# One PSUM tile in place of three, and the next chunk's layer norm ahead of three tiles, in a two-layer recurrent block

## The reference

```python
xn = layernorm(x)                                # layer 0
k, v, r = xn @ Wk.T, xn @ Wv.T, sigmoid(xn @ Wr.T)
kv = k * v                                       # scan over the 4096 positions:
#   wkv_t = state + exp(time_first) * kv_t ; state = decay * state + kv_t
s = (r * wkv) @ Wo.T
h = silu(xn @ wg.T) * (xn @ wu.T)                # 3072 wide, weights int / 127
g = silu(h @ wd.T)
x = x + s * g
xn = layernorm(x)                                # layer 1
diffs = xn[1:] - xn[:-1]                         # 8 of them in a window
normed, mag = diffs / |diffs|, |diffs|
gw = softmax(2 * cos(normed, guidance))          # 512 guidance vectors
blended = 0.6 * normed + 0.4 * gw @ guidance
w = pos_weight * tanh(2 * mag)                   # over the window of 8
s = sum(blended * w) / sum(w)
g = silu(xn @ ternary(weight).T * scale)
out = x + s * g
```

## Time and profile before

| | |
|---|---|
| median of 3 runs | 3196.03 us (3193.56 to 3196.08) |
| the profiled execution: time | 3195.66 us |
| its slowest core (5): span | 3194.1 us |
| spans of the eight cores | 3176.8 to 3194.1 us |
| mean granted clock of TensorE | 0.803 to 0.810 |
| TensorE, weight loads, VectorE, ScalarE, GpSimd busy | 64%, 28%, 32%, 17%, 5% |
| DMA | 291 MB, mean 91 GB/s |

### The profile page before, as it was taken

One profiled execution on the slowest core, in us unless ns is written; L12 is line 12 of the kernel. 1 busy time (PEld: TensorE's weight loads), 2 busy tenths in 40 slices (PEclk: granted clock), 3 DMA queues, 4 the chain that ended last, 5 costly groups with the idle time before them and its releaser, 6 DMA issues.

```text
span 3194.1 us, 24811 instructions; the slowest of 8 cores (3176.8 to 3194.1 us)
## 1 busy us (share of the span) xinstructions
PE 2038.2 (64%) x8803; PEld 894.5 (28%) x8803; DVE 1027.1 (32%) x1856; ACT 552.8 (17%) x925; POOL 148.7 (5%) x83
## 2 busy tenths in 40 slices
PE   3774214697449874598446974498645984479744
PEld 1332101343114331243213431143212432134311
DVE  1420133432334223352335323342233513353232
ACT  1110222111111111111121111111112111211111
POOL 0000000001000010000000010000100000000100
PEclk9887556798669986799778986699867997789867
DMA  7996210531023300342004310233003320043100
GB/s 173 210 207 152 82 50 20 184 111 74 14 92 145 145 1 20 115 156 106 7 20 185 117 68 14 93 145 145 1 20 123 147 106 7 23 155 145 40 14 20
DMA packets 64505, 291.43 MB, mean 91 GB/s; under 512 B 2945, under 2 KB 3458, under 8 KB 58242
## 3 DMA queue, kind: packets, MB, share of 16 engines
q1 hardware_dynamic: 50322, 252.10, 21.3%
q0 software_dynamic: 14064, 37.75, 6.6%
HBM read 273.07 MB, written 44.04 MB: 99 GB/s over the span
## 4 chain that ended last, share of the span: by engine, by line
PE 53%; DVE 16%; DMA 13%; ACT 8%; issue 7%; POOL 3%; DVEq 1%; SPq 0%; ACTq 0%; POOLq 0%
PE pa L53 24%; PE pb L53 18%; PE pc L53 7%; DVE argA L53 6%; PE pt L53 3%; DVE argC L53 3%; DMA ring<-wk_i 3%; ACT argA L53 2%; ACT L53 2%; DMA ring<-wd_i 2%; POOL argA L53 2%; DVE stats L53 2%; ACT argB L53 2%; DVE statL L53 1%; DVE bw L53 1%
## 5 line engine op out<-in xcount | busy, mean ns | idle before, releaser
L53 PE MATMUL pa<-xn0T,ring 128*128 128x512 bf16 x2304 | 574.1, 394 | 119.8 <-DVE argB L53 49.3
L53 PE MATMUL pb<-xn0T,ring 128*128 128x512 bf16 x2304 | 548.2, 381 | 0.0
L53 PEld LDWEIGHTS pa<-xn0T,ring 128*128 128x128 bf16 x2304 | 229.3, 100 | 414.6 <-issue 162.8
L53 PE MATMUL pt<-identb,xnt 128*128 128x128 bf16 x512 | 64.8, 307 | 403.1 <-DVE xnt L53 403.1
L53 PEld LDWEIGHTS pb<-xn0T,ring 128*128 128x128 bf16 x2304 | 227.2, 99 | 279.4 <-issue 13.5
L53 PE MATMUL pa<-ring,argA 128*128 128x512 bf16 x768 | 189.0, 411 | 112.3 <-DMA ring<-wd_i 71.1
L53 PE MATMUL pt<-identb,argA 128*128 128x128 bf16 x352 | 47.1, 305 | 321.6 <-DVE argA L53 292.1
L53 ACT ACTIVATE argC<-pa 128x512 bf16<-128x512 f32 (+1 forms) x112 | 73.7, 658 | 915.8 <-PE pa L53 915.8
L53 ACT ACT_TABLE_LOAD x80 | 102.6, 1283 | 703.2 <-PE pc L53 498.8
L53 PEld LDWEIGHTS pt<-identb,xnt 128*128 128x128 bf16 x512 | 49.6, 138 | 422.6 <-issue 422.6
L53 DVE TENSOR_TENSOR argA<-argC,argB 128x512 bf16<-128x512 bf16 x192 | 81.7, 425 | 264.4 <-ACT argC L53 264.4
(11 more groups left out here) (126 smaller groups left out, 1864.5 us busy)
## 6 DMA issues: line engine op xcount, KB each, us to landing
ring<-wu_i SPq DMA_DIRECT2D x14, 3072.0 KB, 10.8
ring<-wg_i SPq DMA_DIRECT2D x14, 3072.0 KB, 10.7
ring<-wd_i SPq DMA_DIRECT2D x14, 3072.0 KB, 9.9
out<-argA SPq DMA_DIRECT2D x32, 512.0 KB, 2.6
ring<-wk_i SPq DMA_DIRECT2D x7, 2048.0 KB, 14.9
ring<-wv_i SPq DMA_DIRECT2D x7, 2048.0 KB, 19.4
ring<-wr_i SPq DMA_DIRECT2D x7, 2048.0 KB, 7.8
ring<-wo_i SPq DMA_DIRECT2D x7, 2048.0 KB, 7.8
```

Source lines behind the costliest of these rows:

```text
L53: ins = getattr(eng, attr)(*args, **kwargs)
```

## The change

It has three parts.

- In `do_tile` the guidance product and the averaging product no longer use `pa` and `pb` but `pc`, which the ternary product uses as before. The copy out of the averaging product into `tr1` is written ahead of the ternary product, and the ternary product waits for it (`psum_use("pc")`).
- The squares in `do_tile` go to columns 4096 to 5119 of `argB` (the buffer `t1t1` of the down stage) in place of a slot of `sq4`.
- In the chunk loop the statistics of the next chunk's layer norm stand ahead of the three calls of `do_tile`, no longer behind them, and its `ln_apply` stands there too, no longer at the start of the next chunk.

```diff
-        psum_use("pa")
+        psum_use("pc")
         for gi in range(GB):
...
-                E["tensor"].matmul(pa[:, h2 * 512:(h2 + 1) * 512], gwT[:, gi, :],
+                E["tensor"].matmul(pc[:, h2 * 512:(h2 + 1) * 512], gwT[:, gi, :],
...
-        E["vector"].tensor_scalar(t2, pa[:], statL[:, cb + 3:cb + 4], None,
+        E["vector"].tensor_scalar(t2, pc[:], statL[:, cb + 3:cb + 4], None,
...
-        psum_use("pb")
+        psum_use("pc")
         for h2 in range(2):
...
-                E["tensor"].matmul(pb[:, h2 * 512:(h2 + 1) * 512], mprevb[:],
+                E["tensor"].matmul(pc[:, h2 * 512:(h2 + 1) * 512], mprevb[:],
...
         v_rden = R.bump("v")
+        E["vector"].wait(sem_v, v_rden)
+        buf_use("vector", "tr1")
+        E["vector"].tensor_scalar(tr1, pc[:], statL[:, cb + 0:cb + 1], None,
+                                  ALU.mult, _inc=(sem_v, 1))
+        v_tr1 = R.bump("v")
+        psum_set("pc", sem_v, v_tr1)
         psum_use("pc")
         for i in range(DB):
...
         psum_set("pc", sem_a, a_g1)
-        E["vector"].wait(sem_v, v_rden)
-        buf_use("vector", "tr1")
-        E["vector"].tensor_scalar(tr1, pb[:], statL[:, cb + 0:cb + 1], None,
-                                  ALU.mult, _inc=(sem_v, 1))
-        v_tr1 = R.bump("v")
-        psum_set("pb", sem_v, v_tr1)
...
-        buf_use("scalar", "sq_l1")
-        E["scalar"].activation(sq4[:, sl % NT, :], dif_rm, AF.Square,
+        buf_use("scalar", "t1t1")
+        E["scalar"].activation(argB[:, 4096:4096 + D], dif_rm, AF.Square,
...
             rstd0 = ln_finish(0)
-        xn0T_done = ln_apply(xcur, 0, xn0T, rstd0)
-        E["tensor"].wait(sem_v, xn0T_done)
+            xn0_ap_done = ln_apply(xcur, 0, xn0T, rstd0)
+        E["tensor"].wait(sem_v, xn0_ap_done)
...
-        for jt in range(NT - 1):
-            mm = mfirstb if (c == 0 and jt == 0) else mbandb
...
         if c + 1 < NCH:
...
             rstd0 = ln_finish(0)
+            xn0_ap_done = ln_apply(xnx, 0, xn0T, rstd0)
+
+        for jt in range(NT - 1):
+            mm = mfirstb if (c == 0 and jt == 0) else mbandb
```

More of the change, by code:

```diff
@@ L640, in do_tile @@
         buf_use("vector", "t2")
-        E["vector"].tensor_scalar(t2, pa[:], statL[:, cb + 3:cb + 4], None,
+        E["vector"].tensor_scalar(t2, pc[:], statL[:, cb + 3:cb + 4], None,
                                   ALU.mult, _inc=(sem_v, 1))
         v_t2 = R.bump("v")
-        psum_set("pa", sem_v, v_t2)
+        psum_set("pc", sem_v, v_t2)
         E["vector"].wait(sem_v, v_t2)
@@ L652, in do_tile @@
         E["tensor"].wait(sem_v, v_bw)
-        psum_use("pb")
+        psum_use("pc")
         for h2 in range(2):
             kw = {} if (use_prev or h2 == 0) else {"_inc": (sem_t, 1)}
-            E["tensor"].matmul(pb[:, h2 * 512:(h2 + 1) * 512], mmat[:],
+            E["tensor"].matmul(pc[:, h2 * 512:(h2 + 1) * 512], mmat[:],
                                bwc[:, h2 * 512:(h2 + 1) * 512],
@@ L720, in do_tile @@
         buf_set("tg", sem_st, st_c)
-        buf_set("sq_l1", sem_a, a_m2)
+        buf_set("t1t1", sem_a, a_m2)
         pt_seq[0] += 1
@@ L725, in build_fused @@
     rstd0 = None
+    xn0_ap_done = None
     for c in range(NCH):
@@ L984, in build_fused @@
             rstd0 = ln_finish(0)
+            xn0_ap_done = ln_apply(xnx, 0, xn0T, rstd0)
+        for jt in range(NT - 1):
+            mm = mfirstb if (c == 0 and jt == 0) else mbandb
+            useprev = not (c == 0 and jt == 0)
+            do_tile(de[:, :, jt * 128:(jt + 1) * 128], xcur[:, jt, :],
+                    xn1T[:, :, jt * 128:(jt + 1) * 128], mm, useprev,
+                    c * T + jt * 128)
         tlast = R.val("t")
```

## The result

| | before | after |
|---|---|---|
| median of 8 runs | 3195.03 us | 3388.42 us |
| ratio, with its 95% interval | | 1.0605 [1.0593, 1.0617] |
| the profiled execution: time, span of its slowest core | 3195.66, 3194.1 (core 5) | 3388.81, 3387.3 (core 2) |
| mean of the eight spans | 3185.0 | 3379.0 |
| mean granted clock of TensorE, over the cores | 0.806 | 0.768 |

The kernel is 193 us slower; 3393 was forecast. Where a term of a few microseconds is compared I use the mean of the eight spans of the profiled execution, because its cores end up to 17 us apart (3176.8 to 3194.1 us before). The views of the changed kernel are those of core 2.

What follows compares the result with a forecast made beforehand. No engine is full; chains of short waits over each tile and chunk boundary bound the kernel. Terms of 105.6 + 124.9 - 33.0 = 197.5 us on 3195.66 us gave 3393 us, range 3352 to 3432.

Steps and rivals of the forecast that it cites:

- Term 1, the wait: In each of 32 tiles the sixteen ternary matmuls wait until tr1 is read out of pc: 2.4 us later.
- Term 1, the clock: Ternary matmuls behind the hole run partly at 1.2 GHz: 0.9 us more in each of 32 tiles.
- the nearest row: Transposes and dot matmuls after a hole, at clock 0.50 through 4.10 us; low stretch for the ternary matmuls taken as 4.3.
- The rival in which the clock rises as early as before: In the ternary matmuls: the wait costs only 2.40 us a tile, 76.8 in all, 3364 us; chance 13%.
- all sixteen stay low: Rival: all sixteen ternary matmuls run at 1.2 GHz, 4.5 us a tile, 144 in all, 3432 us; chance 5%.
- Term 2, the block: Statistics and normalisation moved ahead of the tiles hide behind nothing: 17.84 us in each of seven chunks, 124.9 us.
- Term 3, the boundary: At seven chunk boundaries wk is issued earlier without the wait for x1prev, so K starts earlier: 33.0 us given back.
- The seventh: Last chunk boundary, with no x to load: wk is there earlier and K starts 9.0 us sooner.
- The sum: Whole kernel: 105.6 + 124.9 - 33.0 = 197.5 us more than 3195.66 us, so 3393 us, 6.2% slower.
- The last rival, K straight behind the last tile: At chunk boundaries K starts straight behind the last ternary matmuls: 216 us gained, 3181 us, not slower; chance 3%.

Runs made afterwards that it cites:

- e9: The changed kernel with the averaging product and tr1 back in pb, guidance and ternary product still sharing pc: 3284.74 to 3292.4 us, ratio 1.0285.
- e3: The changed kernel with five more unused matmuls a tile in the hole ahead of the ternary product: 3332.2 us, ratio to before 1.0403.
- e1: The kernel before with only the do_tile parts of the change, layer norm not moved: 3298.87 and 3298.59 us, ratio to before 1.0296.
- e2: The kernel before with only the moved statistics and normalisation, tiles keeping pa, pb and pc: 3283.84 us, a single run.
- e4: The changed kernel with the next chunk's wk and wv loads issued ahead of the tiles: median 3223.0 us, ratio to before 1.007.
- e5: The kernel before with only the moved norm plus early loads of wk and wv: 3129.12, 3123.46 and 3132.89 us, ratio 0.9792.
- e8: The kernel before with early wk and wv (first chunk: behind guidance and ternary weights), next norm in tile tails, its squares ahead of the first tile: ratio 0.9366.
- run 56: Not a run label: part of the words "made the run 56 us shorter", said of e3, which took 56 us less than the changed kernel.
- e6: The kernel before with early wk and wv and the next norm cut up into the tiles' tails: 3011.72 and 3015.57 us, ratio 0.9434.

## Why the prediction was right

**Term 1, the wait: 2.4 us forecast.** Over 32 tiles the ternary matmuls start 3.90 us behind the first averaging matmul, before 1.48: 2.42 us. That guidance and ternary product share pc free of charge is shown by e9. For guidance and averaging product no run has that alone, but the averaging matmuls wait for bw as long as before, first before, then after (us in total, times, longest):

```profile
PE pb L53 <- DVE bw L53: 101.7, 32, 3.5
PE pc L53 <- DVE bw L53: 102.1, 32, 3.5
```

Tile to tile it is 33.5 us (1709.02 to 1742.52), forecast near 33.6.

**Term 1, the clock: 0.9 us forecast, from a row of another burst, between ends of -1.2 and 2.1.** 5.65 less 4.80 is 0.85 us. The choice of the nearest row was the one guess in the sum, and that it came this close is partly luck: the 32 groups lie anywhere between 4.95 and 6.25 us, and the 4.87 that it was set against came from two tiles. e3 shows that it is idle time and not the shared tile: with the hole filled the clock term turns from a cost of 0.85 into a gain of 0.91 a tile. The term came to 32 x 3.27 = 104.6 us, forecast 105.6. e1 alone gave 105.9 us of mean span. The rival in which the clock rises as early as before (3364 us) falls with it, and so does that in which all sixteen stay low: the last 1.8 us of the tile shown ran at 0.99.

**Term 2, the block: 17.84 us a chunk forecast.** It took from 1257.61 to 1276.13 + 0.69 = 1276.82, 19.2 us, with one table load, and none in the tile behind it. It hid behind nothing: from the ternary matmuls of a chunk's first tile to the next averaging matmul it is 17.8 us longer than before, in the whole change and in e2 alike. The table loads fell from 80 to 66, so Tanh finds SiLU's table too; that gave no time, ScalarE is not late there.

**Term 3, the boundary: 33.0 us forecast.** On the two slowest cores 202.0 less 170.0 us is 32.0 us; in the mean of the eight cores it is 194.3 less 157.5, 36.8 us. wk ends last at all seven. The seventh gave 25.6 - 17.2 = 8.4 for the forecast 9.0. The forecast read one core, and how long wk takes differs between cores.

**The sum.** The mean span rose by 194.0 us and the slowest core's by 193.2, for 197.5 forecast. Measured on all eight cores, in the mean, the parts close: 77.6 (the wait), 26.5 (the longer ternary matmuls), 106.6 (the block in six chunks) and 16.7 (the first chunk up to its first averaging matmul), less 36.8 at the boundaries, and 3.3 elsewhere, most of it between K and the next tiles: 193.9. The first chunk's 16.7 are a block of 17.9 and a start that came 1.1 earlier; on the two slowest cores alone that start came 6.5 us earlier. So the total missed by 3.5 us because the boundary gave 3.8 more than forecast, and the rest nearly cancels.

**The last rival, K straight behind the last tile,** was the right mechanism without its condition. e4 supplies the condition, wk loaded a stage earlier, and K starts with no gap at all; the moved norm then turns from +90 us (e2) into a gain of 2.1% over the kernel before (e5). What the rival lacked in the changed kernel was only where the queue issues wk.

## What to carry to other kernels

Work moved out of one wait has to be priced where it lands, and what else ends late at the place it leaves has to be named: here 19 us moved out of the shadow of a 15 us load, onto a chain with no shadow, to win about 5 a boundary. Move the load first, then cut the work to the size of the holes in the queue that it uses (e8). When two PSUM products share a tile, ask which read now stands ahead of a burst of matmuls, and add the clock to the wait: the hole cost 2.4 us by itself and 0.85 us more behind it.

## What the runs showed of the hardware

- **More matmuls, less time.** In e3 five unused matmuls a tile, 1.9 to 2.3 us together in a hole of 2.15, made the run 56 us shorter than the changed kernel, by keeping TensorE busy nearly until the ternary matmuls came. The Trainium skill, "TensorE: Matmul & The Clock Gate", section "A second HAM failure mode: psum-queue depth-cycling", says that the cost of falling back and warming up again is paid between bursts, and gives no size. The trace agrees, though here the gap is a wait for VectorE within one PSUM tile and not a cycling through banks; the size is 5.65 against 3.89 us for the same sixteen matmuls.
- **A tiny VectorE operation waits for GpSimd.** In e8, in the first tile of each of the six chunks that have it, the statistics' four products, on 128x1 elements, ran beside GpSimd's product:

```profile
1140.47 2.12 POOL L53 TENSOR_TENSOR argA<-argA 128x1024 f32<-128x1024 f32 x1 [34.45 <-ACT argA L53]
1140.81 2.18 DVE L53 SCALAR_TENSOR_TENSOR stats<-stats 128x1 f32<-128x1 f32 x4
1142.92 1.22 DVE L53 TENSOR_TENSOR argA<-argA,x1prev 128x1024 f32<-128x1024 f32 x1
```

 They take 0.61 us alone (the e6 rows) and 2.18 us here (2.49 once); they end 0.4 us behind the GpSimd operation. The sums of 1024 elements a partition did not slow down anywhere (1215 ns before, 1214 in e8), but they did not run beside GpSimd. The Trainium skill, "SBUF — State Buffer", section "Who interferes with whom", says that a VectorE instruction with two SBUF inputs contends with a GpSimd instruction that reads SBUF; the trace agrees. It delayed the add by some 0.2 us here, since it ended with the product that the add waits for anyway.
- **A 2 MB load's time depends on what is queued ahead, and on the core**: wk took 15 us behind x and 9.7 us first in the queue. The guidance load, on another issuing engine's queue, took 8.2 us without and 18.9 us with wk and wv ahead of it. The same wk load had medians of 12.3 to 15.3 us on the cores of one execution; why they differ is not shown.
